# A Fourier-layer tokenizer and four transformer blocks on one core: the layers' loop written out, and the first images loaded inside the preparation

## The reference

```python
h = layer_norm(x @ fc0_w + fc0_b, ln0_g, ln0_b)           # 3 -> 32 channels
h = transpose(h, (0, 3, 1, 2))
for i in range(4):
    w1, w2 = w1r[i] + 1j * w1i[i], w2r[i] + 1j * w2i[i]   # 32 x 32 x 12 x 12 each
    x_ft = rfft2(h)
    out_ft[:, :, :12, :12]  = einsum('bixy,ioxy->boxy', x_ft[:, :, :12, :12], w1)
    out_ft[:, :, -12:, :12] = einsum('bixy,ioxy->boxy', x_ft[:, :, -12:, :12], w2)
    h = irfft2(out_ft) + einsum('bchw,oc->bohw', h, conv_w[i]) + conv_b[i]
    h = layer_norm(h, ln_g[i], ln_b[i])                   # over the channels
    if i < 3: h = gelu(h)
h = gelu(h @ fc1_w + fc1_b); h = gelu(h @ fc2_w + fc2_b); h = h @ fc3_w + fc3_b
```

## Time and profile before

| What | Value |
|---|---|
| Median of three runs | 4603.88 us (4601.17 to 4608.25) |
| The profiled execution | 4607.51 us, its span 4605.7 us |
| PE busy | 3890.6 us, 84% of the span |
| DVE, ACT, POOL busy | 2226.8, 2019.6, 659.7 us |
| PE's first work on images | 230 us after the start |
| Four groups of images | from there to about 3793 us |
| The four blocks behind the tokenizer | from there to the end |

### The profile page before, as it was taken

One profiled execution on the slowest core, in us unless ns is written; L12 is line 12 of the kernel. 1 busy time (PEld: TensorE's weight loads), 2 busy tenths in 40 slices (PEclk: granted clock), 3 DMA queues, 4 the chain that ended last, 5 costly groups with the idle time before them and its releaser, 6 DMA issues. The chain is left out here.

```text
span 4605.7 us, 101008 instructions
## 1 busy us (share of the span) xinstructions
PE 3890.6 (84%) x39477; PEld 2992.3 (65%) x39477; DVE 2226.8 (48%) x4633; ACT 2019.6 (44%) x3050; POOL 659.7 (14%) x444
## 2 busy tenths in 40 slices
PE   0099999998999999989999999899999995686168
PEld 0078888843888888348888872588888625562046
DVE  6544444532454455225445451344544504968756
ACT  1144454466444444654544447454454472221012
POOL 0001221220022122100212230011221300001020
PEclk9999999999999999999999999999999997588579
DMA  8511211110021020102112001020210001000000
GB/s 200 185 27 63 73 34 64 43 56 4 22 84 64 24 82 22 57 2 74 33 64 83 24 22 57 22 65 22 84 64 22 22 3 32 1 1 0 0 1 10
DMA packets 168531, 208.43 MB, mean 45 GB/s; under 512 B 156387, under 2 KB 158664, under 8 KB 159859
## 3 DMA queue, kind: packets, MB, share of 16 engines
q1 hardware_dynamic: 166370, 178.13, 13.5%
q10 hardware_dynamic: 1680, 23.60, 2.1%
HBM read 142.57 MB, written 59.12 MB: 44 GB/s over the span
## 5 line engine op out<-in xcount | busy, mean ns | idle before, releaser
L821 ACT ACTIVATE h<-tp,gb 128x512 f32<-128x512 f32 x640 | 551.3, 867 | 345.2 <-PE tp L493 339.7
L845 POOL TENSOR_TENSOR rstd<-var,mhalf 128x16 f32<-128x16 f32 x192 | 558.7, 2910 | 42.9 <-POOL var L842 42.9
L485 PEld LDWEIGHTS main<-convw,h 128*128 128x128 f32 x3072 | 380.9, 197 | 149.4 <-issue 149.4
L784 DVE TENSOR_REDUCE ssum<-sq 128x16 f32<-128x512 f32 x512 | 345.7, 682 | 273.2 <-ACT sq L809 270.3
L842 POOL TENSOR_TENSOR var<-ssum,eps 128x16 f32<-128x16 f32 x192 | 41.6, 217 | 3018.7 <-DVE ssum L784 3018.7
L534 PE MATMUL main<-fwd_w,pix 128*128 128x96 f32 x4096 | 464.8, 276 | 7.0 <-ACT pix L626 7.0
L534 PEld LDWEIGHTS main<-fwd_w,pix 128*128 128x128 f32 x4096 | 459.8, 192 | 10.2 <-DVE pix L626 8.6
L493 PE MATMUL tp<-ident,xn 128*128 128x128 f32 x2560 | 405.9, 282 | 51.8 <-DVE xn L775 21.5
L485 PE MATMUL main<-convw,h 128*128 (+1 forms) x3072 | 428.6, 288 | 0.0
L452 PE MATMUL aux<-inv_r,yd 96*48 96x64 f32 x8192 | 419.9, 256 | 5.2 <-DVE zq L626 2.3
L452 PEld LDWEIGHTS aux<-inv_r,yd 96*48 96x48 f32 x8192 | 388.8, 185 | 43.3 <-issue 34.7
(11 more groups left out here) (264 smaller groups left out, 5989.4 us busy)
## 6 DMA issues: line engine op xcount, KB each, us to landing
mixw<-mix_scratch SPq DMA_DIRECT2D x15, 4608.0 KB, 15.0
y_scratch<-t_w SPq DMA_DIRECT2D x256, 144.0 KB
yd<-y_scratch SPq DMA_DIRECT2D x32, 1152.0 KB, 7.1
mix_scratch<-mixw SPq DMA_DIRECT2D x64, 288.0 KB, 4.7
mixw<-mix_scratch ACTq DMA_DIRECT2D x1, 4608.0 KB, 13.5
h<-in_L_tok_w1r ACTq DMA_DIRECT2D x6, 576.0 KB, 10.1
h<-in_L_tok_w1i ACTq DMA_DIRECT2D x6, 576.0 KB, 10.2
h<-in_L_tok_w2r ACTq DMA_DIRECT2D x6, 576.0 KB, 18.7
```

What stands on the lines that cost most here:

```text
L485: mm = pe.matmul(bank[:, 128 * i:128 * i + 128], h[:, (u * S + 4 * c + i) * 128:(u * S + 4 * c + i) * 128 + 128], convw[:, layer, :] if l ...
L784: dve.tensor_reduce(ssum[:, c % 4, :], sq[:, c % 2, :].rearrange("p (n c) -> p n c", c=CH), AX.X, ALU.add).then_inc(red_done, 1)
L821: act.activation(out, in_, fn, bias=gb[:, 1, stage:stage + 1] if l is None else gb[:, 1, bass.ds(stage, 1)], scale=gb[:, 0, stage:stage + ...
L845: pool.tensor_tensor(rstd[:, c % 4, :], var[:, c % 4, :], mhalf[:, :], ALU.pow).then_inc(rstd_done, 2)
```

## The change

- The loop over the three layers becomes a Python loop on all five engines: its body stands three times in the program, with `l` a constant. The loop over groups stays.
- DVE's small weights (lines 285 to 309) move from behind the fourth layer to between the reductions and the centring of the second (`n == 1`).
- SP's image loads of the first group, the store of `embw`, the wait for it and both loads of `embw` move to behind the first layer's 16 stores (`n == 0`), ahead of the second layer's.
- The clearing of `xs` goes from DVE at the main block's start to POOL within the preparation, and the waits for it fall away.

```diff
+        def sp_images(sp, g, u):
+            for b in range(NB):
+                for a in range(NA):
+                    img = g * GROUP + (u * UIMG + b * NA + a)
+                    sp.dma_start(xb_of(u)[b:128:2, :].rearrange("r (k a n) -> r a k n", k=8, a=NA)[:, a],
+                                 t["x"][bass.ds(img, 1)].rearrange("a r (k w) c -> r (a k) (w c)", k=8)).then_inc(x_in[u], 16)
...
                         for q in range(4):
                             sp.dma_start(mix_scratch[n][32 * k:32 * k + 32, NK * q:NK * q + NK],
                                          mixw[32 * q:32 * q + 32, NK * k:NK * k + NK]).then_inc(p_store[k], 16)
-                sp.wait_ge(p_done, 3)
-                sp.dma_start(embw_scratch, embw_of(0)).then_inc(p_bstore, 16)
-                sp.wait_ge(p_bstore, 16)
+                    if n == 0:
+                        for u in range(UNITS):
+                            sp_images(sp, 0, u)
+                        sp.wait_ge(p_done, 3)
+                        sp.dma_start(embw_scratch, embw_of(0)).then_inc(p_bstore, 16)
+                        sp.wait_ge(p_bstore, 16)
+                        for u in range(UNITS):
+                            sp.dma_start(embw_of(u), embw_scratch).then_inc(x_in[u], 16)
...
                         dve.tensor_reduce(rsum[:, 2 * (n % 2) + v, :], raw[n % 2][v].rearrange("p (o n) -> p n o", o=CH), AX.X,
                                           ALU.add).then_inc(p_sum, 1)
+                    if n == 1:
+                        dve.wait_ge(p_small, 16 * N_SMALL)
+                        dve.tensor_reduce(bsum, braw, AX.X, ALU.add).then_inc(p_bias, 1)
...
+                        dve.tensor_tensor(embg[:, :].rearrange("p (a w k) -> p a w k", a=NA, k=4),
...
                     dve.wait_ge(p_sum, 2 * (n + 1))
...
-                dve.wait_ge(p_small, 16 * N_SMALL)
-                dve.tensor_reduce(bsum, braw, AX.X, ALU.add).then_inc(p_bias, 1)
...
-                dve.tensor_tensor(embg[:, :].rearrange("p (a w k) -> p a w k", a=NA, k=4),
...
+            @block.gpsimd
+            def _(pool):
+                pool.wait_ge(p_pe, 2)
+                pool.memset(xs[:, :], 0.0)
...
         def sp_x(sp, g, u):
-            for b in range(NB):
...
+            sp_images(sp, g, u)
             sp.dma_start(embw_of(u), embw_scratch).then_inc(x_in[u], 16)
...
                 embed(g)
-                with eng.Fori(0, LAYERS - 1) as l:
+                for l in range(LAYERS - 1):
                     layer(g, l)
...
-                dve.memset(xs[:, :], 0.0).then_inc(xs_zero, 1)
...
-                dve.wait_ge(xs_zero, 1)
...
                 act.dma_start(mixw[:, :], mix_scratch[0]).then_inc(mixw_in, 16)
-                act.wait_ge(xs_zero, 1)
...
-                    with sp.Fori(0, LAYERS - 1) as l:
+                    for l in range(LAYERS - 1):
...
-                for u in range(UNITS):
-                    sp_x(sp, 0, u)
                 with sp.Fori(0, GROUPS - 1) as g:
```

More of the change, by code:

```diff
@@ L210, in tokenizer @@
         gram = sq[0:4, 0, 400:404]
+        x_in = [sem(f"x_in{u}") for u in range(UNITS)]
+        def sp_images(sp, g, u):
[4 more added lines that the diff above has]
+                                 t["x"][bass.ds(img, 1)].rearrange("a r (k w) c -> r (a k) (w c)", k=8)).then_inc(x_in[u], 16)
         with nc.Block() as block:
@@ L271, in _ @@
                                           ALU.add).then_inc(p_sum, 1)
+                    if n == 1:
+                        dve.wait_ge(p_small, 16 * N_SMALL)
+                        dve.tensor_reduce(bsum, braw, AX.X, ALU.add).then_inc(p_bias, 1)
+                        dve.wait_ge(p_bias, 1)
+                        dve.wait_ge(p_zero, 4)
+                        dve.scalar_tensor_tensor(out=biasw[0:LAYERS, 0:CH], in0=bsum.to_broadcast([LAYERS, CH]), scalar=-1.0 / CH, in1=braw,
+                                                 op0=ALU.mult, op1=ALU.add)
+                        dve.tensor_reduce(esum, eraw, AX.X, ALU.add).then_inc(p_done, 1)
+                        dve.wait_ge(p_done, 1)
+                        dve.scalar_tensor_tensor(out=ecen, in0=esum.to_broadcast([4, CH]), scalar=-1.0 / CH, in1=eraw,
+                                                 op0=ALU.mult, op1=ALU.add).then_inc(p_done, 1)
+                        dve.wait_ge(p_pe, 1)
+                        dve.tensor_tensor(embw_of(0).rearrange("p (m o) -> p m o", o=CH),
+                                          mask.unsqueeze(2).to_broadcast([97, 32, CH]),
+                                          aux[0][0:97, 0:CH].unsqueeze(1).to_broadcast([97, 32, CH]), ALU.mult).then_inc(p_done, 1)
+                        dve.wait_ge(p_pe, 2)
+                        for l in range(LAYERS):
+                            for a in range(NA):
+                                dve.tensor_copy(convw[32 * a:32 * a + 32, l, 32 * a:32 * a + 32],
+                                                aux[1][32 * a:32 * a + 32, 32 * l:32 * l + 32])
+                        dve.wait_ge(p_pe, 3)
+                        dve.tensor_copy(etr, tp[0][0:CH, 0:4]).then_inc(p_done, 1)
+                        dve.wait_ge(p_pe, 4)
+                        dve.tensor_scalar(gram, tp[1][0:4, 0:4], 1 / (CH * CUBIC ** 2), None, ALU.mult).then_inc(p_done, 1)
+                        dve.wait_ge(p_pe, 5)
+                        dve.tensor_tensor(embg[:, :].rearrange("p (a w k) -> p a w k", a=NA, k=4),
+                                          mask.rearrange("p (w a) -> p a w", a=NA).unsqueeze(3).to_broadcast([97, NA, 8, 4]),
+                                          main[0][0:97, 0:4].unsqueeze(1).unsqueeze(1).to_broadcast([97, NA, 8, 4]), ALU.mult)
                     dve.wait_ge(p_sum, 2 * (n + 1))
@@ L282, in _ @@
                                 op0=ALU.mult, op1=ALU.add).then_inc(p_cent, 1)
-                dve.wait_ge(p_small, 16 * N_SMALL)
-                dve.tensor_reduce(bsum, braw, AX.X, ALU.add).then_inc(p_bias, 1)
[L286 to L308, removed]
-                dve.tensor_tensor(embg[:, :].rearrange("p (a w k) -> p a w k", a=NA, k=4),
-                                  mask.rearrange("p (w a) -> p a w", a=NA).unsqueeze(3).to_broadcast([97, NA, 8, 4]),
-                                  main[0][0:97, 0:4].unsqueeze(1).unsqueeze(1).to_broadcast([97, NA, 8, 4]), ALU.mult)
             @block.scalar
@@ L362, in tokenizer @@
         turn_full, turn_free = (sem(n) for n in ("turn_full", "turn_free"))
-        mixw_in, xs_zero, y_ready, y_stored = (sem(n) for n in ("mixw_in", "xs_zero", "y_ready", "y_stored"))
-        x_in = [sem(f"x_in{u}") for u in range(UNITS)]
+        mixw_in, y_ready, y_stored = (sem(n) for n in ("mixw_in", "y_ready", "y_stored"))
         yd_in = [sem(f"yd_in{u}") for u in range(UNITS)]
```

## The result

| | Median, us | Runs | Ratio to before, 95% interval |
|---|---|---|---|
| before | 4602.52 | 4600.42 to 4608.25 | |
| after | 4564.72 | 4561.51 to 4572.80 | 0.9919 (0.9901 to 0.9936) |

The change takes off 37.8 us. The predicted time was 4572 us, its range 4548 to 4597: faster as foretold, and 7 us more so.

A forecast was written before the change was run, and what follows sets the result against it. PE bounds the kernel from 230 to about 3793 us, a DVE-SP chain the preparation before it. Loops -47.3 (branches -39.6, table loads -7.7) and preparation +14.4 make -32.9 us: 4572 us, range 4548 to 4597.

The forecast's parts named there:

- Branches: Looped layers: eight branches back per engine cost 4.95 us each in layer length, so -39.6 us.
- only idle time: Looped layers: rival that the loops give only PE's idle time, -29 + 14 = -15, 4589 us; chance 0.10.
- slower: Looped layers: rival that code standing three times must be brought too, loops give nothing, +14 left, 4618 us; chance 0.05.
- Table loads: Unit 0's layer: two ACT table loads cost 0.77 us a body; eight bodies lose both, four one, 7.7 us.
- upper bound: Looped layers: PE's idle time with all of the table loads, 49 us.
- The preparation up to the store: Preparation: small work done at 95.7 us, second centring at 112, sixteen images in 11.9 us, to 111.8.
- The store's hold: Preparation: store of `embw`, on one engine beside ACT's load, keeps SP waiting from 112 to about 152 us.
- the first rival: Preparation: store of `embw` slips through beside ACT's load, ending at 131.5 us; -53, 4551 us; chance 0.12.
- Two loads on one engine: Preparation: both `embw` loads queue on one engine, 30.6 us; third centring 35.4 us after the store, at 187.4.
- on different engines: Preparation: rival that the two `embw` loads run on different engines, 15.3 us less, preparation -1, 4556 us; chance 0.10.
- The rest of the chain: Preparation: DVE needs 47.8 us from the third centring, to 235.2 us; ACT's copy 11.3 us later, at 246.5.
- The base: Whole kernel: profiled execution of before, 4607.5 us, taken as 3.6 us above the median of 4603.9.

## Why the prediction was right, step by step

The direction, the place and most sizes held. In the profiled executions it is -54.3 us for the layers, +8.0 for the preparation and +2.0 for the rest, -44.4 us, where -47.3 and +14.4 were foretold.

- **Branches: held.** Predicted -39.6 us, measured -39.7 with PE's loop alone written out. That the price is read from lengths and not from PE's idle time (29 us) was the step that mattered. The rival "only idle time" fell with this, and so did "slower": with the code standing three times PE is idle for under 1 us in every window of after, and the execution brings 327 pieces of instructions, not 339. In the Trainium skill (Runtime: NRT & Kernel Launch, Instruction fetch mechanics) a taken branch whose target isn't in the current window makes the engine fetch it before it goes on. The rows agree, 3.516 us in the median with eight taken of twelve, 82 ns at least, and so do the instruction transfers of before. In each of the eight taken branches one of 16 KB begins, 0.95 to 1.47 us after the branch, and in none of the four that fall through; over the whole execution one comes every 13.6 us. For the first branch, 546.1 to 549.7 us (packets, MB, share):

```profile
q8 instruction: 1, 0.02, 1.9%
```

So this half of the rival "slower" was right: a fetch of instructions lies in the branch's time. Which engine the packet serves, and how much of the 3.5 us it takes, the trace doesn't tell.

- **Table loads: mis-sized.** I took unit 1's 82.94 us as what unit 0's layer would need without them, so 0.77 us for a body, half of it for each of its two loads. Unit 0's layer needs only 82.5 to 82.7, so 1.0 to 1.2 us were theirs. The error: two layers with other work beside them were treated as one. Nor is it half for each load: the first body keeps the load of line 821 (838 in after) and takes 82.52 us, no more than the bodies with none, 82.49 and 82.73. So the load of line 809 carries it, the one that follows a wait for PE's result. From PE alone to all engines the sum is 1999.3 - 1984.7 = 14.6 us, against 7.7; 13.4 of them lie in unit 0's twelve layers, where 12 x 1.13 us, the gain of the first window with ACT's loop alone, would be 13.6 (an estimate). I also tied the whole to the table loads; the other engines' branches are in the 14.6 too, and no run here parts these. With this term the loops gave 54.3 us, above the 49 that I had set as their upper bound.
- **The preparation up to the store: held.** Small work done at 96.2 us (95.7), second centring done at 112.1 (112), sixteen images 11.61 us (11.9). The store was issued at 109.56 us, 2.2 earlier than assumed, because the first layer's stores ended earlier.
- **The store's hold: right, and 5.5 us too long.** It landed by 146.5 us, not 152. I had put one row of `embw` between two of the load's pieces, and the DMA packets of after bear that out. The store's 97 rows run one by one, 0.155 us each when alone: 26 from 110.6 to 116.0 us, 22 beside the load, the last 49 behind it, from 138.5 to 146.1 us. The two windows 116.05 to 138.45 and 138.45 to 146.4 us show it (packets, MB, share; q1 carries SP's transfers here, and one of the 50 packets is not a row):

```profile
q1 hardware_dynamic: 22, 0.09, 1.7%
q1 hardware_dynamic: 50, 0.20, 6.1%
```

So 22 rows passed where I had put 24. What I had wrong lies at both ends. The store was issued 2.2 us earlier and had 5.4 us before the load reached its engine; the 26 rows of that time (4.0 us) I had not counted. And I had added the store's whole 19.7 us behind the load, with some 4 us of starting and landing in it; of these 0.4 us were left. Against both, the load ended 1.5 us later than I had put. The rule of the Trainium skill (DMA: Bandwidth & Descriptors, Queues, rings and completion order), several descriptors a turn, is not what this transfer did; by it most would have passed. With SP's wait to 146.5 us the first rival (131.5) falls too.

- **Two loads on one engine: held.** 35.2 us from their issue to the third centring, 35.4 predicted. The run with one load shows it: 15.65 us less. The rival "on different engines" falls. By the same page of the Trainium skill (DMA: Bandwidth & Descriptors, Why a DMA increments its semaphore by 16 and not by 1) both should go to the lowest-numbered engine; the runs agree in so far as 97 rows move at 25 GB/s with a share of 0.06, and two such loads take twice as long as one.
- **The rest of the chain: held.** DVE takes the predicted 47.8 us to 229.5, and ACT's copy follows 10.6 us later (11.3).
- **The base.** I allowed 3.6 us for the profiled execution of before; it lies 5.0 above the later median, and that of after 1.6 below its own. So -44.4 us in the spans are -37.8 in the medians. The layers gave 7.0 us more than foretold and the preparation cost 6.4 less, both on the same side. That the forecast missed the median by 7 us and not by 13 is luck: the rest of the execution and the place of the two profiled executions took back the difference.

**What stays open.** In the medians the preparation costs 17.7 us with the loops and 4.2 without (6.6 if each version is set against the before of its own comparison, 4602.5 and 4604.9 us); the traces find 8.8 and 8.4 in the preparation itself. The ratios' intervals reach some 8 us to either side, so the medians don't show that the two costs differ. The first one's lower end, 12 us, lies above 8.8; in its profiled execution the looped layers and "the rest" (MLP, blocks) are 2.0 and 1.9 us longer as well. "The rest" moves by itself: with ACT's loop alone written out it is 2327.1 us, 7.4 under before. No step of the change was found that would explain it.

## What to carry to other kernels

Read the price of a hardware loop's branch from the length of the whole stage with and without it, not from the wait alone; here it was 4.95 us against 3.6. Before a transfer and a wait are put ahead of other stores in a queue, look at how many DMA engines it uses and what runs beside it. A step that fills a gap is worth its place only if what stands behind it in the same queue is not needed first: rows spread over the engines gave 37 us, and the same work behind the stores 12 us more.

## What the runs showed of the hardware

- Each taken branch of the hardware loop on PE's queue had a 16 KB instruction transfer in it (eight of eight, none in the four that fell through), and cost 4.95 us of the stage's length, 3.5 of them the branch.
- A wait of 3.7 us on PE showed in the clock behind it. With the branch the granted clock was 0.73 in the 4 us around it, partly at 1.2 and partly at 2.4 GHz; without it, 1.00 in every window of the layers.
- A transfer of 97 rows of 4 KB moved at 25 GB/s; cut into 96 and one it no longer held SP, and the execution became 37 us shorter. Beside a bulk load of 18 KB rows the wait for it was 36.9 us, alone 17.8; 22 of its rows passed during the 22 us in which that load was on its engine.
- Holding the bulk load back moved that cost to the next one-engine transfers instead of removing it (23.02 us for two issues that took 3.39).
- Stores spread over all engines landed late beside the load too: 18.6 us with nothing of `embw` ahead of them, 26.8 behind its cut loads, where 4.7 was the median.
- Two table loads of 1.283 us stood in a loop body; only the one behind a wait for PE cost time, 1.1 us of the layer.
